# Packing six adjacency tiles under the projection of a graph-attention layer, with the soft steps one tile later

## The reference

```python
h = features @ W                       # 8192 x 256
s1 = h @ a1                            # a1, a2: the halves of attn
s2 = h @ a2
e = leaky_relu(s1[:, None] + s2[None, :], 0.2)
e = where(adjacency > 0, e, -9e15)
attention = softmax(e, axis=1)
h_prime = attention @ h
x = layernorm(x + elu(h_prime))
```

## Time and profile before

| | us |
|---|---|
| median of 3 runs (lowest, highest) | 835.54 (834.55, 835.93) |
| the profiled execution, its own time | 836.63 |
| its span, first to last instruction | 834.90 |
| busy in the span: TensorE, VectorE, ScalarE, POOL | 599.8, 631.7, 572.9, 603.9 |
| share of the span of POOL's gathers (472.8 us busy, 448 of them) | 57% |

### The profile page before, as it was taken

One profiled execution on the slowest core, in us unless ns is written; L12 is line 12 of the kernel. 1 busy time (PEld: TensorE's weight loads), 2 busy tenths in 40 slices (PEclk: granted clock), 3 DMA queues, 4 the chain that ended last, 5 costly groups with the idle time before them and its releaser, 6 DMA issues.

```text
span 834.9 us, 10690 instructions
## 1 busy us (share of the span) xinstructions
PE 599.8 (72%) x2628; PEld 387.7 (46%) x2628; DVE 631.7 (76%) x2422; ACT 572.9 (69%) x529; POOL 603.9 (72%) x688
## 2 busy tenths in 40 slices
PE   6589993468776795877767566678578777876762
PEld 5467771235452462554544333445345344543431
DVE  4568752677789898789988488688787867888776
ACT  0055546687869798878876597678788876797720
POOL 4378524777888877787875787788777876878772
PEclk9699999698989998999999788889798897989967
DMA  8999999799999999999999999999999998999711
GB/s 323 405 398 423 423 420 377 295 419 411 414 414 393 396 416 415 414 415 404 413 417 419 396 353 407 414 352 377 405 411 414 415 415 336 407 416 416 302 32 45
DMA packets 61697, 316.00 MB, mean 378 GB/s; under 512 B 19158, under 2 KB 37815, under 8 KB 45248
## 3 DMA queue, kind: packets, MB, share of 16 engines
q1 hardware_dynamic: 36176, 285.49, 83.7%
q0 software_dynamic: 25456, 29.79, 10.9%
HBM read 340.59 MB, written 17.14 MB: 428 GB/s over the span
## 4 chain that ended last, share of the span: by engine, by line
issue 26%; POOL 21%; DMA 21%; DVE 15%; PE 14%; ACT 1%; POOLq 1%; SPq 0%; ACTq 0%; DVEq 0%
POOL GATH L1549 19%; DMA ADJ<-in_adj_dram 7%; DMA WORK<-in_adj_dram,smalls 6%; PE pk L540 4%; DMA GATH<-haug,ids 3%; DMA X<-in_x_dram 3%; PE spare L524 3%; PE acc L551 2%; PE acc L524 2%; DMA s_row<-WORK 1%; DVE diag L881 1%; PE spare L617 1%; PE xT_ps L513 1%; ACT WORK L1369 1%; DVE smalls L822 1%
## 5 line engine op out<-in xcount | busy, mean ns | idle before, releaser
L1549 POOL DMA_INDIRECT GATH<-haug,ids x448 | 472.8, 1055 | 132.9 <-issue 129.7
L1369 ACT ACTIVATE WORK<-ADJ 128x4096 bf16<-128x4096 int32 x126 | 454.6, 3609 | 101.9 <-PE pk L540 58.0
L540 PE MATMUL pk<-WORK,D 128*128 128x512 bf16 x1024 | 268.0, 413 | 121.6 <-ACT WORK L1369 121.6
L540 PEld LDWEIGHTS pk<-WORK,D 128*128 128x128 bf16 x1024 | 99.8, 103 | 261.5 <-ACT WORK L1369 148.1
L551 PE MATMUL acc<-GATH,diag 128*128 128x256 f32 x512 | 152.5, 451 | 70.3 <-DVE diag L881 70.3
L551 PEld LDWEIGHTS acc<-GATH,diag 128*128 128x128 f32 x512 | 116.8, 233 | 112.1 <-DVE diag L881 87.0
L782 DVE MAX8 smalls<-pk 128x8 f32<-128x512 f32 x64 | 44.5, 695 | 33.5 <-issue 33.5
L891 DVE SCALAR_TENSOR_TENSOR PART<-GATH,smalls,PART 128x256 f32<-128x256 f32 x128 | 62.3, 487 | 4.5
L617 PE MATMUL spare<-X,WORK 128*128 128x256 f32 x256 | 58.7, 383 | 0.0
L860 DVE TENSOR_SCALAR smalls<-GATH,S 128x7 f32<-128x7 f32 x64 | 17.1, 267 | 51.8 <-DMA GATH<-haug,ids 51.6
L617 PEld LDWEIGHTS spare<-X,WORK 128*128 128x128 f32 x256 | 49.3, 193 | 7.0
(11 more groups left out here) (176 smaller groups left out, 808.9 us busy)
## 6 DMA issues: line engine op xcount, KB each, us to landing
ADJ<-in_adj_dram SPq DMA_DIRECT2D x128, 2048.0 KB, 16.5
haug<-GATH POOLq DMA_DIRECT2D x32, 258.0 KB, 11.6
out_dram<-Y SPq DMA_DIRECT2D x32, 256.0 KB, 9.8
GATH<-haug,ids POOLq DMA_INDIRECT x448, 8.5
X<-in_x_dram SPq DMA_DIRECT2D x1, 4096.0 KB, 31.6
X<-in_x_dram SPq DMA_DIRECT2D x1, 3072.0 KB, 25.9
X<-in_x_dram SPq DMA_DIRECT2D x1, 1024.0 KB, 6.5
Waug<-in_L_gnn_W_dram SPq DMA_DIRECT2D x1, 256.0 KB, 2.7
```

The costliest lines, as they stand in the source:

```text
L540: done = nc.tensor.matmul(pk[s % PKS][:], D16[:, k, :], A16[:, q % 2, k * BW:(k + 1) * BW], start=(half == 0 and k == 0), stop=(half == 1 ...
L1369: act.activation(A16[:, q % 2, :], ADJ[:, q % 4, :], ACT.Relu, scale=HALF_SCALE if q % 2 else 1.0, accum_out=degree[:, q // 2, q % 2:q % 2 ...
L1549: pool.indirect_dma_start(out=GATH[:, r, k * DA:(k + 1) * DA], out_offset=None, in_=haug, in_offset=bass.IndirectOffsetOnAxis(ap=ids[:, t ...
```

## The change

Six tiles instead of five are packed under the projection, by twelve packs whose places run up to group 31, the last; packs 2 to 5 move one group forward. The soft steps of the first tiles are one or two steps later (tile 0 in step 7 instead of 6, tile 10 in 17 instead of 15); from tile 44 or so they are as before (tile 63 in step 65 in both). The chunks of round 0 are one step later. The semaphore of the two small stores is split: the gathers and the first exponentials of elu wait for the mean row alone; SP waits for the turned scores at the very end, and POOL before it reads them in the dense part. mid_mark, which writes where the bits of tile 0 lay, waits until all of them are unpacked.

```diff
-EARLY = 5
+EARLY = 6
...
-        extras_stored = sem("extras_stored")
+        mean_stored = sem("mean_stored")
+        s2_stored = sem("s2_stored")
...
         def soft_step(t):
-            return max(math.ceil(5.5 + 0.93 * t), t + 2)
+            return max(math.ceil(7 + 0.905 * t), t + 2)
...
-            return 5 + 3 * x if x < MC else 34 + 3 * (x - MC)
+            return 6 + 3 * x if x < MC else 34 + 3 * (x - MC)
...
-        PACK_AFTER = [8, 10, 13, 15, 17, 19, 21, 23, 25, 27]
+        PACK_AFTER = [8, 10, 12, 14, 16, 18, 21, 23, 25, 27, 29, 31]
...
             sp.wait_ge(mid_stored, 32)
+            sp.wait_ge(s2_stored, 16)
...
             def mid_mark(k):
                 dve.wait_ge(mid_rank_steps, 2)
+                dve.wait_ge(mid_unpacked, 4 * MC)
...
                 if j < 2:
-                    act.wait_ge(extras_stored, 32)
+                    act.wait_ge(mean_stored, 16)
                     act.wait_ge(mean_h_ready, 1)
...
             pool.wait_ge(mean_h_copied, 1)
-            pool.dma_start(haug[N:N + 1, :], mean_row).then_inc(extras_stored, 16)
+            pool.dma_start(haug[N:N + 1, :], mean_row).then_inc(mean_stored, 16)
             pool.wait_ge(s2_copied, 1)
-            pool.dma_start(s2_row, s2T).then_inc(extras_stored, 16)
+            pool.dma_start(s2_row, s2T).then_inc(s2_stored, 16)
             pool.wait_ge(rest_zeroed, 5)
             for b in range(HBS):
                 pool.wait_ge(h_stored[b], 16 * (G // HBS))
-            pool.wait_ge(extras_stored, 32)
+            pool.wait_ge(mean_stored, 16)
...
                 pool.wait_ge(mid_stored, 32)
+                pool.wait_ge(s2_stored, 16)
                 pool.dma_start(s2_all, s2_row.rearrange("t p -> (t p)").partition_broadcast(P)).then_inc(s2_loaded, 16)
```

## The result

The change makes the kernel slower by 0.4%. Over 20 runs of each the median is 840.42 us against 838.32 us before. The ratio estimated from the runs is 1.004 (95% interval 1.0026 to 1.0054); the two medians alone give 1.0025. On the scale of the three runs shown ahead that is 835.54 x 1.004 = 838.9 us (837.6 us by the medians); the forecast was 833.1 us, the range ended at 838.0. By either figure the kernel became slower and not faster. The profiled execution took 840.9 us (span 839.1; before 836.63 and 834.90).

What follows compares the result with a forecast made beforehand. Bounds: the adjacency stream and POOL, both nearly full. The stream gains 2.2 + 4.0 - 1.4 = 4.8 us, but POOL's unmoved end limits this to 2.4: 835.54 - 2.4 = 833.1 us, range 828.5 to 838.0.

Steps and rivals of the forecast that it cites:

- The weak stretch at 124 us: Adjacency loads under the projection: 2.2 us worth of bytes missing, to be covered by loads 16 to 19 going out earlier.
- the two late id waits: POOL's waits of 3.92 and 0.90 us for the ids of tiles 54 and 63, predicted to vanish.
- the wait for the list: POOL's wait before gathering s1, for the ids of the listed rows: predicted 8.5 us behind tile 28, instead of 5.18.
- POOL's run of 670.4 us: POOL's time from first gather to last, less its three waits; predicted unchanged.
- The first gather: Start of POOL's gathers, after h and the mean row land: predicted 134.3 us, range 134.0 to 138.2, against 132.65.
- The first rival: Stores land later beside the earlier loads, first gather at 138.2 us: no change, 836.1 us; chance 0.20.
- The gain on the stream: Adjacency loads come 4.8 us earlier: 2.2 + 4.0 - 1.4, putting the list at 437.95 us.
- the hole: Empty DMA engines from 152 us, 4.0 us, to be covered by two more counted halves except for 1.4 us.
- The sum: POOL's end: first gather 134.3 + run 670.4 + list wait 8.5 = 813.2 us, as before.
- Some 4 us of idle POOL before the gather of tile 14: Longer lags hold tile 10's gather buffer until 278.5 us; POOL's idling there would shorten the list wait by as much.
- The rival that came true: POOL's list wait makes the kernel slower if the stream gains nothing by step 32: 839.5 us; chance 0.18.
- its limit of 440.4 us: Every microsecond the list comes to POOL after 440.4 us is one at the end, with 375.25 us following it.

Runs made afterwards that it cites:

- e3: Changed kernel with load 17 not issued before the mean row has landed: ratio 1.0034 to the kernel before.
- e7: Changed kernel with load 17 held until the mean row landed, round 0's chunks one step earlier, and the gather of s1 behind tile 29: ratio 0.9954.
- e10: Kernel before with only the gathers made free of the turned scores' store (split semaphore): ratio 1.0001.
- e12: Kernel before with split semaphore and longer lags, the gather of s1 kept behind tile 29, five tiles packed: ratio 0.9962.
- e2: Kernel before with the longer lags alone: ratio 1.0017.
- e4: Changed kernel with the chunks of round 0 back at their earlier steps: ratio 1.003.
- e11: Changed kernel run again, unaltered, on another chip: ratio 1.0008 to the kernel before.
- e5: Changed kernel with the gather of s1 one tile later, behind tile 29 as before the change: ratio 0.9955.
- e6: Kernel before with the longer lags and the gather of s1 kept behind tile 29: ratio 0.9954.
- e1: Kernel before with the sixth tile and the twelve packs alone; lags, chunk steps and semaphores as before: ratio 1.0091.
- e9: Kernel before with only the gather of s1 one tile later, behind tile 30: ratio 1.000.

## Why the prediction was wrong

**What held.** The weak stretch at 124 us was filled; ScalarE's wait of 8 us for a pack went; load 20 was issued at 137.1 us; the engines ran dry when the forecast had it (162.6 us; load 21 landed at 162.8); the two late id waits went; the wait for the list moved behind tile 28; POOL's run of 670.4 us was right to 0.1 us, which is in part luck, since it is 667.5 to 673.9 us in the fourteen traces.

**The first gather,** "I take 134.3", with 138.2 us as the far end: it came at 140.99 us, 6.7 us late. The step that failed is the landing of both stores that the gather waits for. For the last store of h the prediction took 13.0 us from an issue at 121.0 us; it was issued at 119.5 us and took 20.6 us, more than the longest of the earlier trace rows. For the mean row it took 9.5 us from an issue at 124.4 us; it was issued at 122.9 us and took 17.8 us. So the packs cost less of TensorE's time than forecast, and the stores much more. The 9.5 us was also too low as a reading (9.5 to 11.4 us), and the earlier trace rows has no load issued between 114.1 and 126.0 us, where the change issues two. The first rival had the mechanism, but stretched only the store of h, and that by too little. e3 and e7 bear it out: with load 17 held the row took 11.8 and 11.3 us, in the five other kernels that pack six tiles 15.8 us or more. It isn't the only cause, as e10 and e12 show (below). The Trainium skill says that DMAs of different engines interleave on the same 16 engines (DMA: Bandwidth & Descriptors, section Issuing engines are not separate DMA queues); the trace agrees, 17.8 us with load 17 beside the row and 11.8 us with it held.

**The gain on the stream,** "4.8 us" by the time of the list: the list came at 441.59 us, 1.16 us earlier than before and not 4.8. The forecast let 1.4 us of the hole stay; 4.5 us stayed, because load 22 went out at 167.4 us and not at 161.1, behind the late first gather. In e3 and e2, with the gate at 135.10 and 131.82 us, the list came at 439.25 and 439.47 us; so of the 3.64 us some 2 go with the late gate, and the rest is a gain that was put too high. This split is an estimate, as e3 has a hole of its own and e2 packs five tiles.

**The end.** The sum failed by its own terms: 6.69 (first gate) - 1.36 (the list wait, 7.14 instead of 8.5) + 0.07 (run) = 5.4 us at POOL's last gather, 818.60 us instead of 813.2 us. The gate's 6.69 us isn't a loss by itself: POOL waits for the list anyway, and a later gate shortens that wait. VectorE took tile 63 4.19 us later than in the earlier trace rows, and the profiled execution was 4.3 us longer:

```profile
821.24 0.22 DVE L862 TENSOR_SCALAR smalls<-GATH,S 128x7 f32<-128x7 f32 x1
```

The forecast had these rows land at 814.6 us. The 6.6 us between are 3.6 us of the later list, 1.8 us of a longer way behind it and 1.2 us of a longer landing of the last gathers.

Some 4 us of idle POOL before the gather of tile 14, which the forecast set off against the list wait, didn't come: POOL was late by more than that. In e2, where it wasn't, POOL waited 6.6 us, but at layernorms.

**The rival that came true** is the one on the list, at a chance of 0.18: its 839.5 us stands against 838.9 us. That the size fits is in part luck. It had the list at 442.75 us, because VectorE would free buffers late, and half of 4.8 us for late id waits; the list came at 441.59 us, in good part for the late first gather of the first rival, and the id waits had gone. Its rule, that behind the list POOL has a fixed way to go, is borne out by the five kernels that wait behind tile 28: the last gather ends 377.0 (after), 376.4 (e2), 376.8 (e3), 373.3 (e4) and 375.9 us (e11) after the list, where the prediction had 375.25. The list times differ by only 3.1 us among the five, though, and the ways by 3.7 us, so the rule isn't tested finely; nor is its limit of 440.4 us, since e2 and e3, with the list before it, are no faster than the kernel before.

The forecast knew of this wait, with 35 tiles behind it instead of 34, and set it off against the two id waits that vanish. What failed is that the offset needed the list at 437.95 us, and no kernel that waits behind tile 28 had it before 439.25 us. What the forecast didn't weigh is that the place of the wait could be left alone: the lags put one more tile of POOL behind the list, seven gathers at 1.3 us each, some 9 us. e5 and e6 take that tile back and gain 0.85% and 0.63%, as differences of ratios (1.004 to 0.9955, 1.0017 to 0.9954). Those ratios come from different chips; by the medians alone it is 4.1 and 2.3 us, 0.5% and 0.3%. On one chip, e12 is 0.6% under the changed kernel (e11), though it also leaves out the packs and the later chunks.

**What the change is worth without that:** -0.45% (e5), and as far as the runs tell all of it comes from the longer lags (e6). Once the lags are long and nobody waits for the list, the late first gate matters little (e5 against e7) and so do the packs with it (e5 against e6); where the lags are short, the packs cost 0.9% (e1). Of the kernels run, e5, e6, e7 and e12 beat the kernel before; the simplest is e6.

**Still open:** why the mean row landed in 12.4 us at most in five of the kernels that pack five tiles and in 15.2 and 19.4 us in e12 and e10, at nearly the same issue times. These two are the ones with the split store, but nothing that they issue before that row differs. They also share a chip, on which e9 had the longest of the five (11.3 to 12.4 us). In e10 the last store of h took 19.9 us too, so it wasn't the row alone. Whether it is chance, the chip or the split was not tried; each is one execution.

## What to carry to other kernels

When a lag is changed, look up every piece of work whose place is found from it: here a wait on another engine moved ahead of one tile, and that cost more than the lag brought. Where two bounds stand level, an edit on either alone shows nothing or less (e9, and e2, which moved the list as well), and their sum shows 0.5% (e6). A store's landing time is a price with its neighbours: where a change brings loads beside it, take it from a row with as many loads. It is also a price that differs from trace to trace (e10), and where two stores share a semaphore, the profile's landing of the first is only a lower bound.

## What had not been expected of the hardware

A store of 1 KB landed in 8.2 to 10.4 us in one kernel (e6) and 19.4 us in another (e10), with the DMA engines moving some 420 GB/s when it was issued in both (422 and 428); the last ten stores of h in the changed kernel took 16.0 to 20.6 us where they took 12.8 to 17.0 us. And the engine that issues the gathers was steady: 448 gathers with all between them, without POOL's waits over 0.8 us, took 667.5 to 673.9 us in fourteen traces, whatever the loads did beside them.
